# TensorE runs one engine loop over both attention layers, the 3x3 convolution under a condition

## Reference

```python
x = L0(x, style, 2, 13)      # Gaussian local mean and std: (x - mean)/std * style std + style mean
x = L1(x, ...)               # attention layer
x = conv3x3(relu(conv3x3(x, w1, b1)), w2, b2) + x
x = L3(x, ...)               # the attention layer again, other weights
```

```python
fl = ln(patches)                                       # 64 x 1024
pf = attn(fl @ Wqk_p) @ pv + dwconv(pv);  pv = fl @ Wv_p
pf = merge(pf) @ Wout_p
ww = softmax(ln(pooled) @ Wqk_w ...)                   # 4 x 4 per head; its diagonal scales pf
wv = ln(windows) @ Wv_w                                # Wv_w: 16384 x 1024
wf = merge(nds @ wv + dwconv(wv)) @ Wout_w             # Wout_w: 1024 x 16384
out = diag * pf + wf + x
```

## Time and profile before

| | us |
|---|---|
| median of 3 runs | 749.94 (749.78 to 750.79) |
| the profiled execution | 749.65 |
| its span, first to last instruction | 747.8 |
| PE busy / DVE / ACT | 434.6 / 91.2 / 38.2 |
| DMA queue of the loads, share of 16 engines | 99.3% |
| mean DMA rate | 429 GB/s |
| mean granted TensorE clock | 0.772 of full |

### The profile page before, as it was taken

One profiled execution on the slowest core, in us unless ns is written; L12 is line 12 of the kernel. 1 busy time (PEld: TensorE's weight loads), 2 busy tenths in 40 slices (PEclk: granted clock), 3 DMA queues, 4 the chain that ended last, 5 costly groups with the idle time before them and its releaser, 6 DMA issues.

```text
span 747.8 us, 6863 instructions
## 1 busy us (share of the span) xinstructions
PE 434.6 (58%) x3011; PEld 128.6 (17%) x3011; DVE 91.2 (12%) x254; ACT 38.2 (5%) x80; POOL 9.3 (1%) x21
## 2 busy tenths in 40 slices
PE   5698944445445455455586988544544464454457
PEld 5333200000001111111122332000000021111113
DVE  4756100000002000000005171000000020000000
ACT  2111100000000000000001010000000000000000
POOL 2100000000000000000001000000000000000000
PEclk9589877767777776776788999777777787777779
DMA  9999999999999999999999999999999999999997
GB/s 392 446 397 444 441 449 410 435 445 424 435 431 446 414 436 438 449 417 428 429 447 435 410 436 441 428 442 438 431 424 445 431 429 435 438 428 428 445 408 324
DMA packets 7928, 320.57 MB, mean 429 GB/s; under 512 B 1049, under 2 KB 1585, under 8 KB 2153
## 3 DMA queue, kind: packets, MB, share of 16 engines
q1 hardware_dynamic: 7913, 320.35, 99.3%
HBM read 319.86 MB, written 0.49 MB: 428 GB/s over the span
## 4 chain that ended last, share of the span: by engine, by line
DMA 64%; PE 31%; DVE 3%; ACT 1%; issue 1%; SPq 0%; DVEq 0%; ACTq 0%
DMA ring<-halves 60%; PE bank L489 10%; PE bank L515 9%; PE bank L407 4%; DMA ring<-last 4%; PE bank L424 2%; PE bank L416 2%; PE bank L539 1%; PE bank L387 0%; PE bank L334 0%; PE bank L316 0%; DMA cst<-blurs 0%; DVE ring L722 0%; PE bank L378 0%; PE bank L537 0%
## 5 line engine op out<-in xcount | busy, mean ns | idle before, releaser
L489 PE MATMUL bank<-ring,stage 128*4 128x512 f32 x1024 | 141.9, 717 | 143.5 <-DMA ring<-halves 143.5
L515 PE MATMUL bank<-ring,wf_t 128*32 128x512 f32 x960 | 137.7, 738 | 125.7 <-DMA ring<-halves 125.7
L489 PEld LDWEIGHTS bank<-ring,stage 128*4 128x4 f32 x1024 | 27.2, 97 | 258.0 <-DMA ring<-halves 157.3
L515 PEld LDWEIGHTS bank<-ring,wf_t 128*32 128x32 f32 x960 | 33.4, 133 | 219.7 <-DMA ring<-halves 129.0
L935 DVE TENSOR_TENSOR image<-bank,image 128x32 f32 (+1 forms) x30 | 5.1, 193 | 275.9 <-PE bank L316 275.9
L900 DVE COPY wv_t<-bank 128x32 f32<-128x32 f32 x2 | 0.4, 192 | 290.1 <-PE bank L316 290.1
L316 PE MATMUL bank<-ident,area 128*128 128x128 f32 (+1 forms) x117 | 18.3, 284 | 14.5 <-ACT area L656 11.1
L656 ACT COPY area<-bank 128x512 f32<-128x512 f32 x15 | 8.8, 585 | 279.6 <-PE bank L515 279.6
L407 PE MATMUL bank<-extra,area 128*64 128x512 f32 x64 | 19.3, 771 | 1.9 <-DVE area L809 1.9
L473 PE MATMUL bank<-extra,area 128*64 128x512 f32 x64 | 18.5, 743 | 1.8 <-DVE area L874 1.8
L316 PEld LDWEIGHTS bank<-ident,area 128*128 128x128 f32 (+1 forms) x117 | 12.5, 141 | 34.0 <-ACT area L656 23.8
(11 more groups left out here) (202 smaller groups left out, 206.5 us busy)
## 6 DMA issues: line engine op xcount, KB each, us to landing
extra<-ends SPq DMA_DIRECT2D x4, 4096.0 KB, 17.0
ring<-halves SPq DMA_DIRECT2D x4, 4096.0 KB, 21.3
ring<-last SPq DMA_DIRECT2D x1, 3072.0 KB, 21.3
ring<-last SPq DMA_DIRECT2D x2, 1536.0 KB, 24.6
ring<-last SPq DMA_DIRECT2D x1, 1024.0 KB, 27.6
ring<-last SPq DMA_DIRECT2D x1, 768.0 KB, 28.7
ring<-halves SPq DMA_DIRECT2D x33, 29.5
ring<-images SPq DMA_DIRECT2D x1, 512.0 KB, 3.5
```

Of the source, the lines that this page charges most:

```text
L489: m = mm(bank[0][32 * j:32 * j + 4, :], stage[:, k // 8, at:at + 4], w[:, j], start=False, stop=False)
L515: m = mm(bank[6 + g][32 * j:32 * j + 32, :], wf_t[:, h, :], w[:, j], start=(h == 0), stop=(h == GROUP - 1))
```

## The change

PE's Python loop over the layers becomes an engine loop over `L` (a register), the convolutions stand under `pe.If(L < 1)`, and the small matmul of the convolution weights moves ahead of the loop. Waits for `vec_copied` and `l2_rep_copied`, which stood in layer 0 alone, now stand in both. Thresholds that were constants (`L + 1`, and those of `half_there`) come from registers. The wait for `wf_ready` moves into the first group of each turn. Two small matmuls behind `nds_ready` change places. The other engines' programs stay as they are.

```diff
+            pe.wait_ge(l2_landed, 16)
+            mm(bank[7][:, 0:N_L2], cc("repeat", C), l2[:, :], start=True, stop=True).then_inc(l2_repeated, 1)
+
-            for L in range(2):
+            with pe.Fori(0, 2) as L:
                 pe.wait_ge(image_ready, L + 1)
                 mm(bank[0][:, :], ones, pixels, start=True, stop=True).then_inc(sums, 1)
                 pe.wait_ge(py_ready, L + 1)
-                if L == 0:
-                    pe.wait_ge(vec_copied, 1)
+                pe.wait_ge(vec_copied, 1)
...
-                if L == 0:
-
-                    pe.wait_ge(l2_landed, 16)
-                    mm(bank[7][:, 0:N_L2], cc("repeat", C), l2[:, :], start=True, stop=True).then_inc(l2_repeated, 1)
...
-                if L == 0:
-                    pe.wait_ge(l2_rep_copied, 1)
+                pe.wait_ge(l2_rep_copied, 1)
...
-                turn(bank[3][0:32, 288:320], ww[:, 2, :], rows=32)
-                mm(bank[3][:, 320:321], cc("spread", 32), wstat[:, 4:5], start=True, stop=True).then_inc(nds_turned, 1)
+                mm(bank[3][:, 320:321], cc("spread", 32), wstat[:, 4:5], start=True, stop=True)
+                turn(bank[3][0:32, 288:320], ww[:, 2, :], rows=32).then_inc(nds_turned, 1)
...
-                pe.wait_ge(wf_ready, L + 1)
-                def group(i, g):
+                def group(L, i, g):
                     for h in range(GROUP):
+                        if h == 0 and g == 0:
+                            pe.wait_ge(wf_ready, L + 1)
                         if h == 0:
                             half_there(L, i + TURNS, g)
...
                 with pe.Fori(0, TURNS - L) as i:
                     for g in range(2):
-                        group(i, g)
+                        group(L, i, g)
                         turn_group(i * 2 + (2 * TURNS * L + g + 1), g)
-                if L == 0:
+                with pe.If(L < 1):
...
-            group(TURNS - 1, 0)
+            group(1, TURNS - 1, 0)
```

## The result

The changed kernel takes 748.66 us in the median of 22 runs (748.43 to 750.08), the kernel before 749.79 us in 22 runs beside it (749.48 to 750.79). The ratio is 0.9986, with a 95% interval of 0.998 to 0.9991: **1.1 us faster**, outside the noise. The forecast was no change at 749.9 us, range 748.9 to 751.8.

A forecast was written before the change was run, and what follows sets the result against it. The prediction took the stream of weights as the bound. To the profiled 749.65 us it added 0 each for matmul, register thresholds (0.15 within the free delay), branch and end; the forecast was the median, 749.9 us, range 748.9 to 751.8.

The forecast's parts named there:

- What bounds the kernel: Whole kernel: the stream of weights is the bound, 319.86 MB taking 742 us; PE matters only where the stream runs dry.
- free delay of 0.8 to 1.3 us at the layer change: Layer change: PE may be this much later before the nearly empty load queue leaves DMA engines without work.
- the formula: Layer change: a delay d beyond 3.6 us costs about d less 2.2 us; one between costs a part.
- moved matmul: Layer 0's front: the small matmul makes the sums at most about 0.4 us later, covered by queued loads, cost 0.
- The branch: Way back to layer 1: 0.5 us at most, hidden by about 3.5 us of cover, cost 0.
- register thresholds: Layer change: register operations and sequencer waits add 0.15 us on the path, bounds 0 and 0.3, within the free delay.
- Rival 1: Way back to layer 1: a fetch, hidden or nearly, 749.9 to 751.0 us; visible part below 1.5 us, chance 0.17.
- chances of 0.68 and 0.17: Way back: 0.68 for no fetch or a hidden one with no change, 0.17 for a visible part below 1.5 us.
- Rival 2: Way back: two fetches in a row, then TensorE at the lower clock; delay 5.3 us, time 753.0 us, chance 0.09.
- 1.7 us for the clock: Behind two fetches on the way back: a 1.7 us term in the 5.3 us delay, with TensorE at the lower clock.
- Fewer instructions: PE's program: five fewer fetches give the stream 5 x 1.1 / 16 = 0.3 us back, gain bounded by 0 and 0.3.
- rival 3: Whole stream: faster, about 748 us, needing another stream rate; 0.3 us of fewer fetches can't be measured; chance 0.06.

The follow-up runs named there:

- Experiment 4: The changed kernel with the `Wv_w` turns written out inside the layer loop, a body of about 2,040 instructions: 751.38 us.
- experiment 1: The changed kernel with the layer loop and the condition written out again in Python, every other edit kept: 749.87 us.
- experiment 6: The changed kernel with two extra loads of 17 rows of 4 KB in SP's queue, behind the second half of layer 1's first loads: 754.87 us.
- 7: The changed kernel with two extra loads of 16 rows of 4 KB in SP's queue, behind the second half of layer 1's first loads: 750.48 us.
- 10: The changed kernel with an extra load of 17 rows of 1 KB on ACT's queue in each of layer 1's four `Wv_w` turns: 750.47 us.
- 11: The changed kernel with an extra load of 16 rows of 1,088 bytes on ACT's queue in each of layer 1's four `Wv_w` turns: 749.69 us.
- experiments 2 and 3: The kernel before with turn loops written out, first those of `Wv_w`, then all four: 752.91 us and 752.03 us.

## Why the prediction was wrong

**What bounds the kernel** was right: the stream sets the end, and PE's own time didn't matter.

**The free delay of 0.8 to 1.3 us at the layer change** was never called on. SP issued `extra` at 418.41 us, a little before the 419 to 420 forecast: 13.6 us after the landing at 404.81, where it had been 14.6 us (419.11 after 404.48). Experiment 4 is the check. There it was 17.1 us (423.12 after 406.04), a delay of 2.5 us, for which the formula allows a few tenths. The stream did run dry: the 16 steps of `extra`'s load came within 0.5 us of each other, where they had been spread over 2.2, and their mean came 1.8 us later than in the stream without a hole. But the last came only 0.1 us later, since the slowest engine still had work. So the formula isn't confirmed: it priced the engines in the mean, and the slowest one sets the landing.

**The moved matmul** came out as priced. PE's instructions in order of time:

```profile
23.80 1.97 PE L370 MATMUL bank<-ident,ring 128*64 128x64 f32 x32 [6.91 <-DVE ring L726]
25.71 1.33 PE L375 MATMUL bank<-l,cst 16*128 16x290 f32 x2
26.97 2.08 PE L380 MATMUL bank<-image,ones 128*128 128x512 f32 x2
```

From L370's end to L380 it is 26.97 - 25.77 = 1.20 us where it was 0.89: 0.3 us on that path (0.4 forecast), and none at the end, by experiment 1.

**The branch and the register thresholds** were right at 0: 216 ns, 5.4 us ahead instead of the 3.5 us assumed, and 42 to 56 ns for each of the register operations of L326. **Rival 1** didn't occur, by 8 fetches and by the 0.04 us before L380: the way back over about 1,260 instructions took 216 ns and needed no fetch (what the prediction calls "the loop's pages" are its packets of 16 KB, one a fetch). No run before it showed that; the chances of 0.68 and 0.17 were the author's estimate. Experiment 4 puts the limit between about 1,260 and about 2,040 instructions. **Rival 2** didn't occur either. No run shows its 1.7 us for the clock: it is the difference between the 20.8 us from L378's start to the end of L407's part on `extra` in layer 0, at a granted clock of 0.60, and the 19.1 us from L378's start to the issue of `extra` in layer 1, at 0.73. Behind the fetch of 8.2 us in experiment 4 the second of these stretches took 19.0 us (404.11 to 423.12) at 0.73, as before.

**The step that failed** is "Fewer instructions": "Five fewer would give the stream 5 x 1.1 / 16 = 0.3 us back", which then was put at 0 in the sum. That fewer fetches help the stream stood in the prediction, and the count was near (four). The size was off by more than 3: 1.1 us. The division by 16 is what was wrong. It would hold if the other engines took over the work of the one that is held. They don't: the distances among the 16 steps, the same within some 0.02 us from load to load, show that a load's shares are fixed and that an engine put back stays back. A fetch put its engine back by 1.5 us where that can be read (464.30 and 614.22 us in the kernel before, 464.78 in experiment 1), more than the 1.0 to 1.1 us of its packet and the 1.3 us of the expectations. Four such fetches make 4 x 1.5 / 16 = 0.38 us in the mean, which is just what the mean of the 16 gained; the landing gained 1.16.

Of the four fetches saved, the one at 464.30 us carries 0.9 us, since it met an engine 0.6 us ahead of the slowest. The one at 614.22 met an engine 1.60 us ahead, moved it to 0.06 us ahead, and cost nothing. The other two, at 421.57 and 442.25, are worth 0.1 us together. And 0.15 us come from a fetch at 240 us that both kernels make: it met an engine with 1.4 us of head start before and with 1.6 now. Which engine a fetch meets decides its price, and nothing that the prediction read shows it; so that the gain came out at 1.1 us, and not nearer to nothing, is in part luck. From the division by 16 followed the second error, the sentence of rival 3 that the 0.3 us "can't be measured", and the chance of 0.06 for faster. That the engines finish apart from each other is shown by the 16 steps of each large load, which lie up to 3.1 us apart at 473.60 us in the kernel before, and by experiment 6, where one of them is 4.5 us behind the rest.

What stays open: the trace doesn't name the engine of a packet; that each of the 16 steps is one engine is read from their distances, which stay the same over a dozen loads. The steps are those of one profiled execution of each kernel, in which the last piece landed 0.75 us earlier than before (743.53 instead of 744.28), while the medians differ by 1.1. That the loop is the cause is shown by experiment 1; that it acts through the engine that a fetch puts back is shown by the 16 steps and by the two pairs 6 and 7, 10 and 11. Why experiments 2 and 3 lost over 2 us in their first 56 us is not known, nor why a fetch puts its engine back by more than its packet takes.

## What to carry to other kernels

In a kernel bound by a stream of large loads, price anything that holds a single DMA engine (here a fetch of 16 KB, or the loads of 17 rows, 4.4 us dearer than those of 16) by its full time on that engine (1.5 us for a fetch here) against the head start that the engine has over the slowest: between nothing and all of it, and not by a sixteenth. A rolled loop over whole layers can then pay by its fewer fetches alone (1.1 us for four here), as long as its body isn't fetched again: about 1,260 instructions weren't, about 2,040 were, and the branch back then took 8.2 us. A branch whose wait stands behind it, not ahead of it, cost nothing here, where the sequencer ran ahead of the matmuls (216 ns, done 5.2 us before L380).

## What was not expected of the hardware

- The one branch that waited for a fetch took 8.17 us under a full stream (experiment 4), though the packet of 16 KB itself takes 1.1 us and a small load at the idle start 3.4 us.
- A fetch put one engine back by 1.5 us, and the engine didn't make it up: after the fetch at 464.30 us the distances among the 16 steps are the same at 473.60 and, but for the one at 614.22, at 725.18.
- Small loads cost more than their bytes between or beside large ones here: two of 65 KB in 16 rows 1.8 us instead of 0.3, four of 17 KB in 16 rows 1.0 us instead of 0.16.
- A row more made the small loads far dearer: 4.4 us between two kernels that load 131 KB in 16 rows and 139 KB in 17.
